# Two graph-attention layers on one core: one exponential per attention weight, two source tiles of ten as split one-pass products, and attention sums of `w2` moved one stage later

## The chip, the cores and the metric

The kernel runs on one core of a Trainium2 chip. The metric is the device time of one execution in microseconds (us), the median over several runs; lower is better. The engines are TensorE (PE, with its weight loads shown apart as PEld), VectorE (DVE), ScalarE (ACT), GpSimd (POOL) and SyncE (SP, here only a DMA queue).

## The reference, cut to what matters

A graph of 1250 nodes and 20000 edges plus a loop at each node passes two blocks, each followed by a layer normalization. The first block holds three attention convolutions of four heads with 192 features each:

```
h = (x1 @ W).reshape(N, H, C)                 # N=1250, H=4, C=192, three times
e = leaky_relu(as_n[src] + ad_n[dst], 0.2)    # as_n, ad_n: h times a_src, a_dst, summed
p = exp(e - segment_max(e, dst))
out = segment_sum(p / segment_sum(p, dst) * h[src], dst) + b
x = layernorm(x + relu(concat(relu(out)) @ W_out + b_out))
```

The second block is one such convolution of four heads with 512 features (weights `w1`), an ELU and one of a single head (weights `w2`).

## The kernel before

Nodes stand in `NT = 10` tiles of `T = 125`. The edge list has been turned into a dense matrix of counts `CT` (source by destination), so an aggregation over edges is a dense product: for each head and each source tile, a matrix `p` of 125 sources by 1250 destinations is built and multiplied with the 125 rows of `h`. The stages run one after another, each a block with a barrier behind it: counts and `x1`, `project` (h and the scores, and for each head the rows `u`, `v` per destination), `aggregate_layer0`, `project_out_layer0`, then the same for the second block.

**`aggregate_layer0` (L897).** 6 iterations of 2 heads, 20 steps each, 120 steps in all; a step is one source tile `s` of one head `hh`.
- ACT (L1048 to L1052) writes two exponentials per step, of `u` plus a source column and of `v` plus a scaled source column, 1250 wide, into a ring of 4. It may run 4 steps ahead of `p`.
- DVE (L1086 to L1094) takes the larger of the two (L1088), waits for itself, then takes min with 1 and multiplies by the counts into `p`, also a ring of 4 (L1093). Exponentials of two exponents, of which the larger is taken, are the leaky ReLU inside the exponential.
- PE (L1132 to L1143) multiplies: for each of 10 destination tiles a float32 product of 125x125 (stationary `p`) with 125x193 (193rd column of `h`: ones, which yields the sum of `p`). Such a product is recorded as two matmuls. The results of one head fill 5 PSUM banks, two destination tiles each. There is no second set of banks.
- So at each change of heads: DVE reads the sums and inverts them (`divisors`, L1071, called after step 1 of the next head, first for two banks and then for three), ACT scales the 10 results out of PSUM (`leave_head`, L1012, after the exponentials of step 3), and PE's first products of the next head wait for the bank. After two heads PE transposes the results in three chunks (`turn`, L1112, behind steps 1, 3 and 5 of the next iteration), ACT adds the bias (`keep`, L1025).
- In 16 of the first 110 steps, every seventh, DVE does two more reductions behind L1093: products of a chunk of `w2` (128 rows x 768) with the attention vectors of the last layer, summed (`ScoreWeights.reduce`, L634). POOL's queue loads these chunks.

**`project_out_layer0` (L1790).** 20 pieces (10 node tiles, two halves of the 18 chunks of 128), each 54 one-pass products of 384 columns with both operands split into a rounded part and a rest (float32r). Per piece ACT rounds and DVE forms the rest (`rest_of_f`, two buffers); per node tile DVE adds, normalizes (`leave`) and sums two or three chunks of `w1` with its attention vectors (`sums`, 24 chunks of 128x512 in a ring of 2, loaded by POOL's queue, the vectors once per 6 chunks).

Of the kernel before, what the change touches and what calls it, by code (L numbers as in the profile page):

```python
# [640 lines left out]
def project(nc, core, xT, w, wa, h_rows, score_rows, width, col_src, u_col, v_col):  # L641
# [12 lines left out]
    with ExitStack() as ctx:  # L654
# [111 lines left out]
        def _(dve):  # L766
# [5 lines left out]
            v.tensor_copy(col_src[0][:, 0:heads, :], score[:, 0])  # L772
# [124 lines left out]
def aggregate_layer0(nc, core, h_rows, col_src, bias, turned_rows, w2, a2, w_out):  # L897
# [9 lines left out]
    RING = 4  # L907
    with ExitStack() as ctx:
# [5 lines left out]
        e = sb("e", [T, RING, 2, N], F32)  # L914
        p = sb("p", [T, RING, N], F32)
        res = sb("res", [T, NT, PAIR], F32)
# [13 lines left out]
        more_ready = sem("more_ready")  # L930
        p_ready = sem("p_ready")
        p_used = sem("p_used")
        banks_done = sem("banks_done")
# [7 lines left out]
        weighed = ScoreWeights(nc, sb, sem, "wa2_by", 2, D // 2, 2, K1, K1, 1)  # L941
# [3 lines left out]
        def _(pool):  # L945
# [6 lines left out]
            by_half = w2.rearrange("(u g) (k p) c -> g k p u c", g=2, p=128)  # L952
            weighed.loads(pool, lambda n: by_half[n // (K1 // 2), n % (K1 // 2)],
                          lambda g: a2.rearrange("(u g) a c -> g u a c", g=2)[0:1].broadcast_to([128, 2, 2, D // 2]))
# [7 lines left out]
        def _(sp):  # L962
            sp.dma_start(b_col[:], bias).then_inc(bias_in, 16)

            def load(i):
                for s in range(2):
                    if (i, s) == (0, 0):
                        continue
                    wait_apart(sp, exp_ready, i * STEPS + (s + 1) * NT)
# [36 lines left out]
        def _(act):  # L1006
# [32 lines left out]
            def body(i, first):  # L1039
                for g in range(STEPS):  # L1040
                    hh, s = divmod(g, NT)
                    if s == 0:
                        if g == 0:
                            wait_apart(act, core.first_uv_in if first else uv_in[0], 64 if first else i * 64)
                        else:
                            wait_apart(act, uv_in[1], i * 64 + 64)
# [19 lines left out]
        def _(dve):  # L1066
            v = nc.vector
            v.sem_inc(p_ready, RING)
            v.sem_inc(exp_ready, 2 * NT)
# [12 lines left out]

            def body(i, first):
                for g in range(STEPS):
                    hh, s = divmod(g, NT)
                    dve.wait_ge(exp_ready, i * STEPS + (g + 1 + 2 * NT))  # L1086

                    v.tensor_tensor(e[:, g % RING, 0, :], e[:, g % RING, 0, :], e[:, g % RING, 1, :], ALU.max).then_inc(more_ready, 1)  # L1088
                    dve.wait_ge(more_ready, i * STEPS + (g + 1))

                    dve.wait_ge(p_used, i * STEPS + (g + 1 + 2 * NT - RING))

                    v.scalar_tensor_tensor(p[:, g % RING, :], e[:, g % RING, 0, :], 1.0, CT[:, s, :],  # L1093
                                           ALU.min, ALU.mult).then_inc(p_ready, 1)  # L1094
                    if (i * STEPS + g) % 7 == 4 and (i * STEPS + g) // 7 < K1:
                        k = (i * STEPS + g) // 7
                        weighed.reduce(dve, k, lambda kind, j: core.wa2[:, k, kind:kind + 1])
# [9 lines left out]
        def _(pe):  # L1107
# [16 lines left out]
            def body(i, first):  # L1124
                for g in range(STEPS):
# [6 lines left out]
                    pe.wait_ge(p_ready, i * STEPS + (g + 1 + RING))  # L1132
                    for d in range(NT):
                        b, n = divmod(d, 2)
                        if s == 0 and n == 0:

                            pe.wait_ge(bank_free, i * (2 * BANKS) + (BANKS * hh + b + 1))
                        last = nc.tensor.matmul(p_o[:, b, n * 256:n * 256 + C0 + 1], p[:, g % RING, d * T:(d + 1) * T],  # L1138
                                                h_in[hh][:, s, 0:C0 + 1], start=(s == 0 and n == 0), stop=(s == NT - 1),
# [650 lines left out]
def project_out_layer0(nc, core, turned_rows, w, x, bias, x2_rows, w1, a1):  # L1790
# [9 lines left out]
    with ExitStack() as ctx:  # L1800
# [129 lines left out]
        def _(dve):  # L1930
# [750 lines left out]
```

## Time and profile before

| | us |
|---|---|
| median of 3 runs | 1923.69 (1923.25 to 1928.69) |
| profiled execution, its own time | 1930.16 |
| its span | 1928.4 |
| PE busy | 1839.7 (95%) |
| DVE busy | 1443.6 (75%) |
| ACT busy | 1030.9 (53%) |
| POOL busy | 142.1 (7%) |

The span counts from the first to the last instruction that was recorded; the time holds some microseconds around it. Matmuls overlap, so that their duration says less than the distance from the start of one to the start of the next. "Idle before" an engine's instruction comes with the instruction that released it.

### The profile page before, as it was taken

The numbers are of one execution on the slowest core, as the hardware profiler recorded it, in microseconds if no ns is written. First come the engines' busy times: TensorE is split into PE (matmuls) and PEld (weight loads), VectorE is DVE, ScalarE is ACT, GpSimd is POOL, SyncE is SP. The second block draws the span as 40 slices with busy tenths as digits, with TensorE's granted clock in tenths as the row PEclk, the third lists the DMA queues.
The fourth block names the chain that finished last, engine by engine and source line by source line (L and its number), as shares of the span: only waits on it lengthen the run. The fifth ranks groups of instructions, "written<-read, shape, count | busy, mean of one in ns | idle before, by whom it ended". The sixth has DMA issues, their size and how long they took to land. (4 is left out here: it accounts for less than half of the span.)

```text
span 1928.4 us, 30682 instructions
## 1 busy us (share of the span) xinstructions
PE 1839.7 (95%) x11399; PEld 1776.6 (92%) x11399; DVE 1443.6 (75%) x2468; ACT 1030.9 (53%) x1634; POOL 142.1 (7%) x139
## 2 busy tenths in 40 slices
PE   7999999998999999998999999989999998999998
PEld 5877699998999999988999999989999998999997
DVE  8888599998888988965465549457888886346766
ACT  4676412218898889864211322257778875232632
POOL 5100211201000000000111011100000000000000
PEclk9999999999999999999999999989999999999989
DMA  4221335355455436619644466462342406544302
GB/s 126 67 64 54 99 103 149 101 133 142 134 111 131 108 77 149 145 16 248 185 141 143 135 208 188 141 193 79 108 143 66 138 28 204 156 129 126 99 9 80
DMA packets 179273, 234.12 MB, mean 121 GB/s; under 512 B 75943, under 2 KB 151655, under 8 KB 178889
## 3 DMA queue, kind: packets, MB, share of 16 engines
q1 hardware_dynamic: 170407, 202.98, 38.5%
q0 software_dynamic: 7984, 27.24, 4.9%
q10 hardware_dynamic: 748, 2.10, 0.4%
q8 instruction: 86, 1.41, 0.3%
q14 instruction: 48, 0.39, 0.1%
HBM read 167.27 MB, written 65.00 MB: 120 GB/s over the span
## 5 line engine op out<-in xcount | busy, mean ns | idle before, releaser
L1755 PE MATMUL p_o<-p_hi,h_parts 125*128 125x416 f32 (+1 forms) x960 | 283.0, 356 | 7.4 <-DVE z L1676 6.1
L1138 PE MATMUL p_o<-first_room,p 125*125 125x193 f32 x1200 | 202.2, 329 | 6.2 <-ACT res L1020 2.9
L1138 PEld LDWEIGHTS p_o<-first_room,p 125*125 125x125 f32 x1200 | 197.1, 189 | 8.0 <-issue 6.7
L1138 PE MATMUL p_o<-h_in,p 125*125 125x193 f32 x1200 | 200.9, 330 | 3.6 <-ACT res L1020 3.6
L1138 PEld LDWEIGHTS p_o<-h_in,p 125*125 125x125 f32 x1200 | 198.7, 190 | 5.0 <-issue 3.8
L1755 PEld LDWEIGHTS p_o<-p_hi,h_parts 125*128 125x128 f32 x960 | 182.0, 190 | 13.7 <-DVE z L1676 10.1
L781 DVE CUSTOM_DVE_ANT_0 max_junk<-src_row,G 125x1250 bf16<-125x1250 f32 x120 | 184.8, 1612 | 3.6 <-ACT src_row L819 1.5
L885 PE MATMUL p_h<-pw_hi,x1T 128*125 128x384 f32 x720 | 187.3, 341 | 0.0
L1088 DVE TENSOR_TENSOR e<-e 125x1250 f32<-125x1250 f32 x120 | 174.3, 1453 | 17.2 <-ACT e L1050 17.1
L1474 PE MATMUL p_h<-pw_hi,x2T 128*125 128x256 f32 (+1 forms) x960 | 177.8, 287 | 3.9 <-DVE h_out L1430 3.9
L1093 DVE SCALAR_TENSOR_TENSOR p<-e,CT 125x1250 f32<-125x1250 f32 x120 | 175.3, 1461 | 5.7 <-PE p_o L1138 1.7
L1755 PE MATMUL p_o<-p_lo,h_parts 125*128 125x416 f32 (+1 forms) x480 | 169.9, 354 | 0.0
L1050 ACT ACTIVATE e<-first_room,col 125x1250 f32<-125x1250 f32 x120 | 151.1, 1344 | 6.9 <-DVE p L1093 5.5
L1474 PEld LDWEIGHTS p_h<-pw_hi,x2T 128*125 128x125 f32 x960 | 150.4, 190 | 4.2 <-DVE h_out L1430 4.1
L1050 ACT ACTIVATE e<-uv,col 125x1250 f32<-125x1250 f32 x120 | 149.0, 1349 | 1.2 <-DVE p L1093 1.2
L1474 PE MATMUL p_h<-pw_lo,x2T 128*125 128x256 f32 (+1 forms) x480 | 136.9, 285 | 0.0
L885 PEld LDWEIGHTS p_h<-pw_hi,x1T 128*125 128x125 f32 x720 | 131.7, 188 | 1.2 <-issue 1.2
L2012 PE MATMUL p_y<-fw_hi,f_hi 128*125 128x384 f32 x360 | 121.9, 339 | 4.2 <-DVE fw_lo L1935 4.1
L885 PE MATMUL p_h<-pw_lo,x1T 128*125 128x384 f32 x360 | 122.5, 340 | 0.0
L2012 PE MATMUL p_y<-fw_lo,f_hi 128*125 128x384 f32 x360 | 121.6, 338 | 0.0
L2012 PE MATMUL p_y<-fw_hi,f_lo 128*125 128x384 f32 x360 | 121.5, 337 | 0.0
L481 PE MATMUL p_count<-src_hot,dst_hot 125*125 125x416 bf16 (+1 forms) x588 | 112.7, 350 | 6.3 <-DVE dst_hot L286 6.3
(285 smaller groups left out, 3839.3 us busy)
## 6 DMA issues: line engine op xcount, KB each, us to landing
f_raw<-turned SPq DMA_DIRECT2D x40, 500.0 KB, 8.8
h_parts<-h_rows SPq DMA_DIRECT2D x40, 448.0 KB
turned<-tail_room SPq DMA_DIRECT2D x18, 625.0 KB, 6.9
G<-turned SPq DMA_DIRECT2D x20, 562.5 KB
h_rows<-tail_room SPq DMA_DIRECT2D x22, 424.4 KB
h_rows<-h_out SPq DMA_DIRECT2D x16, 560.0 KB
h_rows<-tail_room SPq DMA_DIRECT2D x14, 560.0 KB
first_room<-in_w_gat POOLq DMA_DIRECT2D x36, 192.0 KB, 2.7
```

The source lines that it names most:

```text
L481: last = nc.tensor.matmul(p_count[:, i, 0:w], dst_hot[:, h, :], src_hot[:, h, a:a + w], start=False, stop=False, skip_group_check=True)
L781: v.tensor_tensor_reduce(out=junk[:, t % 2, :], in0=src_row[:, h % 2, :], in1=G[:, t, :], scale=1.0, scalar=NO_EDGE, op0=ALU.subtract, op1 ...
L885: last = nc.tensor.matmul(p_h[:, (u * NT + t) % 4, 0:width], xp[:, k, at], wp[:, u, k, :], start=(k == 0 and n == 0), stop=(k == KD - 1 an ...
L1050: last = a.activation(e[:, g % RING, kind, :], uv[hh][:, kind, :], ACT.Exp, bias=col_src[kind][:, bass.ds(i * 2 + hh, 1), s])
L1088: v.tensor_tensor(e[:, g % RING, 0, :], e[:, g % RING, 0, :], e[:, g % RING, 1, :], ALU.max).then_inc(more_ready, 1)
L1093: v.scalar_tensor_tensor(p[:, g % RING, :], e[:, g % RING, 0, :], 1.0, CT[:, s, :], ALU.min, ALU.mult).then_inc(p_ready, 1)
L1138: last = nc.tensor.matmul(p_o[:, b, n * 256:n * 256 + C0 + 1], p[:, g % RING, d * T:(d + 1) * T], h_in[hh][:, s, 0:C0 + 1], start=(s == 0 ...
L1474: last = nc.tensor.matmul(p_h[:, n % 4, 0:width], xp[:, k, at], wp[:, q % 2, k, 0:width], start=(k == 0 and j == 0), stop=(k == KD - 1 and ...
L1755: last = nc.tensor.matmul(p_o[:, bank(n, c), 0:w], h[:, s, kind, cols].bitcast(F32R), pp[:, g % RING, 0:w], start=(s == 0 and j == 0), sto ...
L2012: last = nc.tensor.matmul(p_y[:, t % 2, half, 0:CW], fp[:, n % 2, kk, :], wp[:, k, cols], start=(k == 0 and j == 0), stop=(k == KO - 1 and ...
```

## The change

- In `aggregate_layer0` DVE takes the larger exponent before the exponential: `larger_exponent(n)` adds the source column to `u` and takes the larger of that and `v` in one instruction, two steps ahead of `p` (`AHEAD = 2`). ACT then does one exponential per step, in place. The column of `u` is scaled by 1 - SLOPE in `project`, and the exponential's bias is the column times SLOPE.
- For source tiles 4 and 8 of each head the product is made of float32r parts: ACT rounds `p` and these two tiles of `h`, DVE subtracts, and PE does three products of 194 columns in the place of one float32 product.
- The sums over `w2` leave this stage. They are done in `project_out_layer0`: 32 chunks of 128x384 in two halves, in a ring of 2, four chunks per node tile from tile 1 to 8, with one instruction at the end that adds the halves. POOL's queue loads them in turn with those of `w1`.

```diff
-            v.tensor_copy(col_src[0][:, 0:heads, :], score[:, 0])
+            v.tensor_scalar(col_src[0][:, 0:heads, :], score[:, 0], 1 - SLOPE, None, ALU.mult)
...
@@ aggregate_layer0, scalar
-                    wait_apart(act, p_ready, i * STEPS + (g + 1))
-                    for kind in range(2):
-                        last = a.activation(e[:, g % RING, kind, :], uv[hh][:, kind, :], ACT.Exp,
-                                            bias=col_src[kind][:, bass.ds(i * 2 + hh, 1), s])
-                    last.then_inc(exp_ready, 1)
+                    wait_apart(act, larger, i * STEPS + (g + 1 + 2 * NT))
+                    a.activation(e[:, g % RING, :], e[:, g % RING, :], ACT.Exp,
+                                 bias=col_src[1][:, bass.ds(i * 2 + hh, 1), s]).then_inc(exp_ready, 1)
+                    n = i * STEPS + g
+                    if in_parts(n - 1) is not None:
+                        m = in_parts(n - 1)
+                        if m >= 2:
+                            act.wait_ge(p_used, step_in_parts(m - 2) + 1 + 2 * NT)
+                        act.wait_ge(p_ready, n + RING)
+                        a.activation(p_hi[:, m % 2, :], p[:, (n - 1) % RING, :], ACT.Copy).then_inc(p_hi_ready, 1)
+                    if s == 1:
...
+                        a.activation(h_hi[:, hh], h_in_parts(hh), ACT.Copy).then_inc(h_hi_ready, 1)
@@ aggregate_layer0, vector
+            def larger_exponent(n):
...
+                dve.wait_ge(p_ready, n + 1)
+                v.scalar_tensor_tensor(e[:, n % RING, :], uv[hh][:, 0, :], col_src[0][:, i * 2 + hh, s:s + 1], uv[hh][:, 1, :],
+                                       ALU.add, ALU.max).then_inc(larger, 1)
...
-                    dve.wait_ge(exp_ready, i * STEPS + (g + 1 + 2 * NT))
-                    v.tensor_tensor(e[:, g % RING, 0, :], e[:, g % RING, 0, :], e[:, g % RING, 1, :], ALU.max).then_inc(more_ready, 1)
-                    dve.wait_ge(more_ready, i * STEPS + (g + 1))
+                    dve.wait_ge(exp_ready, i * STEPS + (g + 1))
                     dve.wait_ge(p_used, i * STEPS + (g + 1 + 2 * NT - RING))
-                    v.scalar_tensor_tensor(p[:, g % RING, :], e[:, g % RING, 0, :], 1.0, CT[:, s, :],
+                    v.scalar_tensor_tensor(p[:, g % RING, :], e[:, g % RING, :], 1.0, CT[:, s, :],
                                            ALU.min, ALU.mult).then_inc(p_ready, 1)
-                    if (i * STEPS + g) % 7 == 4 and (i * STEPS + g) // 7 < K1:
-                        k = (i * STEPS + g) // 7
-                        weighed.reduce(dve, k, lambda kind, j: core.wa2[:, k, kind:kind + 1])
+                    if i * STEPS + g + AHEAD < ITERS * STEPS:
+                        larger_exponent(i * STEPS + g + AHEAD)
+                    n = i * STEPS + g
+                    if in_parts(n - 1) is not None:
+                        m = in_parts(n - 1)
+                        dve.wait_ge(p_hi_ready, m + 1)
+                        v.tensor_tensor(p_lo[:, m % 2, :], p[:, (n - 1) % RING, :], p_hi[:, m % 2, :].bitcast(F32),
+                                        ALU.subtract).then_inc(p_split, 1)
+                    if s == 2:
+                        dve.wait_ge(h_hi_ready, i * 2 + hh + 1)
+                        v.tensor_tensor(h_lo[:, hh], h_in_parts(hh), h_hi[:, hh].bitcast(F32), ALU.subtract).then_inc(h_split, 1)
@@ aggregate_layer0, tensor
+                        if m is None:
...
+                        else:
+                            for pp, hp in ((p_hi, h_hi), (p_hi, h_lo), (p_lo, h_hi)):
+                                last = nc.tensor.matmul(p_o[:, b, n * 256:n * 256 + HC0], pp[:, m % 2, nodes], hp[:, hh, m % EACH, :],
+                                                        start=False, stop=False, skip_group_check=True)
@@ project_out_layer0, gpsimd
+            pool.wait_ge(w_split, KO)
+            for t in range(1, NT):
+                for n in w1_chunks(t):
...
+                for m in w2_chunks(t, 0, 4):
...
+                    if m >= 2:
+                        pool.wait_ge(w2_summed, 2 * (m - 1))
+                    pool.dma_start(w2_ring[:, m % 2], w2[2 * half + k // (K1 // 2), k % (K1 // 2) * 128:(k % (K1 // 2) + 1) * 128, :]
+                                   ).then_inc(w2_in[m % 2], 16)
@@ project_out_layer0, vector
             for t in range(2, NT):
                 rest_of_f(2 * t)
                 sums(t - 1)
+                sums_of_w2(t - 1, 0, 2)
                 rest_of_f(2 * t + 1)
                 leave(t - 1)
+                sums_of_w2(t - 1, 2, 4)
             sums(NT - 1)
             leave(NT - 1)
+            dve.wait_ge(w2_summed, 4 * K1)
+            v.tensor_tensor(core.wa2[:], core.wa2[:], wa2_half[:], ALU.add)
```

## Rows read from the trace of the kernel before

**Rows 1.** The page, part 1: busy us, share of the span, instructions.
```profile
PE 1839.7 (95%) x11399; PEld 1776.6 (92%) x11399; DVE 1443.6 (75%) x2468; ACT 1030.9 (53%) x1634; POOL 142.1 (7%) x139
```

**Rows 2.** Stretches: first aggregation, a stretch inside it, output projection.
```profile
core 0: us, PE busy (x) PEld busy (x) DVE busy (x) ACT busy (x) POOL busy (x), PEclk, DMA share, GB/s
...
479.00:484.00 5.00, 5.00 (x17) 5.00 (x16) 4.93 (x5) 5.00 (x9) 0.00 (x0) 0.50 1.04 253
...
881.00:1078.00 197.00, 192.20 (x1096) 191.09 (x1097) 109.58 (x237) 46.43 (x55) 19.49 (x28) 1.00 0.56 169
438.00:862.00 424.00, 415.45 (x2550) 411.79 (x2550) 375.07 (x350) 353.56 (x396) 12.12 (x17) 0.99 0.47 113
```

**Rows 3.** Costliest groups of the first aggregation: count, busy us, mean ns, idle before.
```profile
L1138 PE MATMUL p_o<-first_room,p 125*125 125x193 f32 x1200 | 202.2, 329 | 6.2 <-ACT res L1020 2.9 <-issue 2.9 <-DVE p L1093 0.5
...
L1093 DVE SCALAR_TENSOR_TENSOR p<-e,CT 125x1250 f32<-125x1250 f32 x120 | 175.3, 1461 | 5.7 <-PE p_o L1138 1.7
...
L634 DVE CUSTOM_DVE_ANT_1 wa_by_junk<-wa_by_w,wa_by_a 128x768 bf16<-128x768 f32 x32 | 29.3, 952 | 2.6 <-DMA wa_by_w<-in_w 2.6
```

**Rows 4.** Timeline of engines: start us, us, instructions merged; transposes, and float32 products undisturbed.
```profile
520.71 1.23 PE L1120 MATMUL p_t<-ident,res 125*128 125x125 f32 x10
...
639.82 10.46 PE L1138 MATMUL p_o<-h_in,p 125*125 125x193 f32 x63
```

**Rows 5.** Timeline of the last stage: 256 columns, then weight loads of 2-column products.
```profile
1851.79 0.51 PE L2532 MATMUL p_ol<-h_lo_l,p_hi_l 125*125 125x256 f32 x3
1852.14 0.51 PE L2532 MATMUL p_ol<-h_hi_l,p_lo_l 125*125 125x256 f32 x3
...
1855.58 1.18 PEld L2540 LDWEIGHTS p_ol<-ones_l,G 125*125 125x125 f32 x10
```

**Rows 6.** Instructions of L2540: duration ns, min/median/max.
```profile
L2540 PEld LDWEIGHTS p_ol<-ones_l,G x20: 185/189/190, 1855.6 to 1897.2; 125*125 125x125 f32 x20
```

**Rows 7.** DVE's timeline in an undisturbed stretch of the first aggregation.
```profile
482.02 1.46 DVE L1093 SCALAR_TENSOR_TENSOR p<-e,CT 125x1250 f32<-125x1250 f32 x1
483.40 1.45 DVE L1088 TENSOR_TENSOR e<-e 125x1250 f32<-125x1250 f32 x1
484.89 1.46 DVE L1093 SCALAR_TENSOR_TENSOR p<-e,CT 125x1250 f32<-125x1250 f32 x1
```

**Rows 8.** DVE groups by form, whole span: scalar from a constant, from a column.
```profile
L1698 DVE SCALAR_TENSOR_TENSOR e<-e,CT 125x416 f32<-125x416 f32 x80 | 47.4, 593 | 2.8
...
L1683 DVE SCALAR_TENSOR_TENSOR tail_room<-z,b_col,tail_room 128x416 f32<-128x416 f32 x28 | 18.1, 646 | 0.0
```

**Rows 9.** Timeline of the first aggregation's start.
```profile
433.93 12.39 ACT L1050 ACTIVATE e<-first_room,col 125x1250 f32<-125x1250 f32 x10 [1.25 <-DVEq L1068]
...
438.03 1.46 DVE L1093 SCALAR_TENSOR_TENSOR p<-e,CT 125x1250 f32<-125x1250 f32 x1
...
439.59 6.65 PE L1138 MATMUL p_o<-first_room,p 125*125 125x193 f32 x29 [2.85 <-issue]
```

**Rows 10.** Timeline of the first change of heads, with `w2` sums in DVE's queue.
```profile
475.38 0.95 DVE L634 CUSTOM_DVE_ANT_1 wa_by_junk<-wa_by_w,wa_by_a 128x768 bf16<-128x768 f32 x1
...
477.13 0.16 DVE L1077 TENSOR_SCALAR sums<-p_o 125x4 f32<-125x4 f32 x1
...
478.48 7.71 PE L1138 MATMUL p_o<-h_in,p 125*125 125x193 f32 x29 [3.56 <-ACT res L1020]
```

**Rows 11.** Timeline of PE: a wait inside a head, and a later change of heads.
```profile
458.31 1.90 PE L1138 MATMUL p_o<-first_room,p 125*125 125x193 f32 x10 [0.47 <-DVE p L1093]
...
584.06 4.16 PE L1138 MATMUL p_o<-first_room,p 125*125 125x193 f32 x24 [0.96 <-ACT res L1020]
```

**Rows 12.** DVE's timeline in the output projection, three of its waits and the reductions.
```profile
990.28 1.33 DVE L1939 TENSOR_TENSOR f_lo<-G,f_hi 128x1125 fp32r<-128x1125 f32 x1 [3.58 <-ACT f_hi L1904]
...
1000.88 0.69 DVE L634 CUSTOM_DVE_ANT_1 tail_room<-tail_room 128x512 bf16<-128x512 f32 x1 [6.83 <-DMA tail_room<-in_a]
...
1003.36 0.96 DVE L1950 TENSOR_TENSOR p_y<-p_y,tail_room 125x768 f32<-125x768 f32 x1
...
1007.85 0.16 DVE L1973 SCALAR_TENSOR_TENSOR ln_shift<-ln_moments,ln_better 125x1 f32<-125x1 f32 x1
...
1019.30 0.69 DVE L634 CUSTOM_DVE_ANT_1 tail_room<-tail_room 128x512 bf16<-128x512 f32 x1 [5.39 <-DMA tail_room<-in_w]
```

More of the change, by code:

```diff
@@ L907, in aggregate_layer0 @@
     RING = 4
+    AHEAD = 2
+    IN_PARTS = (4, 8)
+    EACH = len(IN_PARTS)
     with ExitStack() as ctx:
@@ L913, in aggregate_layer0 @@
         uv, h_in = (uv_first, uv_other[:]), (h_first, h_other[:])
-        e = sb("e", [T, RING, 2, N], F32)
+        e = sb("e", [T, RING, N], F32)
         p = sb("p", [T, RING, N], F32)
+        p_hi = sb("p_hi", [T, 2, N], F32R)
+        p_lo = sb("p_lo", [T, 2, N], F32R)
+        h_hi = sb("h_hi", [T, 2, EACH, HC0], F32R)
+        h_lo = sb("h_lo", [T, 2, EACH, HC0], F32R)
         res = sb("res", [T, NT, PAIR], F32)
@@ L929, in aggregate_layer0 @@
         exp_ready = sem("exp_ready")
-        more_ready = sem("more_ready")
+        larger = sem("larger")
         p_ready = sem("p_ready")
         p_used = sem("p_used")
+        p_hi_ready = sem("p_hi_ready")
+        p_split = sem("p_split")
+        h_hi_ready = sem("h_hi_ready")
+        h_split = sem("h_split")
         banks_done = sem("banks_done")
@@ L951, in _, with in_parts, step_in_parts, h_in_parts @@
                            core.h0_late)
-            by_half = w2.rearrange("(u g) (k p) c -> g k p u c", g=2, p=128)
-            weighed.loads(pool, lambda n: by_half[n // (K1 // 2), n % (K1 // 2)],
-                          lambda g: a2.rearrange("(u g) a c -> g u a c", g=2)[0:1].broadcast_to([128, 2, 2, D // 2]))
+        def in_parts(n):
+            return n // NT * EACH + IN_PARTS.index(n % NT) if n % NT in IN_PARTS else None
+        def step_in_parts(m):
+            return m // EACH * NT + IN_PARTS[m % EACH]
+        def h_in_parts(hh):
+            return h_in[hh][:, IN_PARTS[0]:IN_PARTS[-1] + 1:IN_PARTS[1] - IN_PARTS[0], :]
         def every_iteration(eng, body):
@@ L968, in load @@
                         continue
-                    wait_apart(sp, exp_ready, i * STEPS + (s + 1) * NT)
+                    wait_apart(sp, larger, i * STEPS + (s + 1) * NT)
                     wait_apart(sp, p_used, i * STEPS + (s + 1) * NT)
@@ L1068, in _ @@
             v.sem_inc(p_ready, RING)
-            v.sem_inc(exp_ready, 2 * NT)
+            v.sem_inc(larger, 2 * NT)
             def divisors(i, hh):
@@ L1081, in divisors @@
                     v.reciprocal(sums[:, 1, 2 * b0:2 * b1], sums[:, 0, 2 * b0:2 * b1]).then_inc(sum_steps, 1)
+            def larger_exponent(n):
+                i, g = divmod(n, STEPS)
+                hh, s = divmod(g, NT)
+                if s == 0:
+                    if n == 0:
+                        dve.wait_ge(core.first_uv_in, 64)
+                    else:
+                        dve.wait_ge(uv_in[hh], i * 64 + 64 * hh)
+                dve.wait_ge(p_ready, n + 1)
+                v.scalar_tensor_tensor(e[:, n % RING, :], uv[hh][:, 0, :], col_src[0][:, i * 2 + hh, s:s + 1], uv[hh][:, 1, :],
+                                       ALU.add, ALU.max).then_inc(larger, 1)
+            for n in range(AHEAD):
+                larger_exponent(n)
             def body(i, first):
@@ L1832, in project_out_layer0 @@
         w1_in = sem("w1_in")
+        w2_in = [sem(f"w2_in{r}") for r in range(2)]
+        a2_in = sem("a2_in")
+        w2_summed = sem("w2_summed")
+        w1_chunks = lambda t: range(weighed.chunks * (t - 1) // (NT - 1), weighed.chunks * t // (NT - 1))
+        w2_chunks = lambda t, a, b: range(4 * (t - 1) + a, 4 * (t - 1) + b) if t < NT - 1 else ()
         block = ctx.enter_context(nc.Block())
@@ L1975, in sums, with sums_of_w2 @@
             def sums(t):
-                for n in range(weighed.chunks * (t - 1) // (NT - 1), weighed.chunks * t // (NT - 1)):
+                for n in w1_chunks(t):
                     weighed.reduce(dve, n, lambda kind, j: core.wa1[:, n % KD, kind, n // KD:n // KD + 1])
+            def sums_of_w2(t, a, b):
+                for m in w2_chunks(t, a, b):
+                    half, k = divmod(m, K1)
+                    if k == 0:
+                        dve.wait_ge(a2_in, 16 * (half + 1))
+                    dve.wait_ge(w2_in[m % 2], 16 * (m // 2 + 1))
+                    for kind in range(2):
+                        if 2 * m + kind:
+                            dve.wait_ge(w2_summed, 2 * m + kind)
+                        to = (core.wa2 if half else wa2_half)[:, k, kind:kind + 1]
+                        v.tensor_tensor_reduce(out=w2_junk[:], in0=w2_ring[:, m % 2], in1=a2_now[:, kind], scale=1.0, scalar=0.0,
+                                               op0=ALU.mult, op1=ALU.add, accum_out=to).then_inc(w2_summed, 1)
             rest_of_f(0)
```

58 lines of the change are left out of this document (42 added, 16 removed).

## The prediction

> **What bounds the kernel now.** I read the page first: PE is busy for 95% of the span, DVE for 75% [rows 1]. Then the stretches. The first aggregation (438 to 862 us) is PE's: 2550 matmul records fill 415 of 424 us, while DVE is busy for 375 us, 88% of it [rows 2]. DVE is second by so little that what it does late shows up in PE. Where it does, I took from the idle time before L1138 and from the timeline around each place:
> - a product step (one source tile) is 20 records. 63 records last 10.46 us, less the last one's 0.33 this is 10.13/62 = 0.1634 us per record, 3.27 us per step [rows 4]. 120 steps are 392 us, and 15 groups of transposes of (1.23 - 0.27) x 10/9 = 1.07 us are 16 us more [rows 4].
> - DVE's step is 1.38 us from L1093 to L1088 and 1.49 from L1088 to L1093, since the second waits for the first, 2.87 in all [rows 7]; per head 28.7, with two divisors of 0.35 each 29.4, and the `w2` sums, 16 x 1.8 us over 12 heads, another 2.4: 31.8 against PE's 32.7 in a head without transposes.
> - the `w2` sums fall where they hurt. At 475.38 two of them stand ahead of the divisors; ACT can't empty a bank, and PE idles 3.56 us [rows 10]. The clock falls behind it: from 479 to 484 us it is granted at 0.50, 1.2 GHz, and 17 records stand where 31 would [rows 2], 14 x 0.1634 = 2.3 us in that stretch, about 2.8 with its edges. At 458.31 PE waits 0.47 for `p`, and at three changes of heads (584.06 is one) 0.96 [rows 11].
>
> **The products in parts.** Removed in 24 steps: 20 records, 3.27 us. Added: 30 products of 194 columns, each with its own weight load of 125 columns. The trace has no such product. From above: 256 columns, also one pass, start 0.35/3 = 0.118 us apart [rows 5]. From below by the columns: the same scaled by 194/256 is 0.089. But weight loads have a pace of their own: ahead of products with only 2 columns, ten loads take 1.18 us, less one duration of 0.19 this is 0.99/9 = 0.110 us each [rows 5, 6]. Two columns can't hold anything up, so this is the load. I take 0.109: 30 x 0.109 = 3.27 us, and 24 steps give 0. Ends: 0.118 gives +0.27 x 24 = +6.5, 0.089 gives -0.60 x 24 = -14.4, of which DVE lets through what follows below.
>
> The Trainium skill has a rule for either side ("TensorE: Matmul & The Clock Gate"). Its section on the back-to-back issue gap puts a warm product at N/2.4 + 2.5 ns, for 194 columns 83 ns; that would be 2.50 us per step and -18 us. Its section on LDWEIGHTS puts a load at P/1.2, 104 ns for 125 columns. The 0.110 of the row speaks for the second as the floor here.
>
> **The larger exponent.** Removed: L1088, 120 x 1.45 us, and the wait behind it. Added: a two-operand instruction of the same 1250 elements with its scalar from a column. With a column L1683 takes 646 ns where L1698 with a constant takes 593, both 416 elements [rows 8]: +0.05. So 1.38 + 0.05 = 1.43 per step, and `p` 1.38: 2.81 where it was 2.87. The bounds are 1.38 and 1.49 for either instruction. ACT drops from two exponentials of 1.24 us (12.39 for 10) [rows 9] to one, 150 us less, beside its work for the parts (24 x 1.3 for `p`, 12 x 0.5); ACT bounds nothing, so this is worth 0.
>
> **DVE's head after.** 10 x 1.38 + 10 x 1.43 + two rests of `p` of 1.38 + the rest of `h` (388 elements, by the 416 of [rows 8] 0.5) + divisors 0.7 = 32.1 us, against PE's 32.7 plainly and 35.9 with transposes. DVE and PE are all but equal in seven heads. Two chains decide:
> - At the change of heads the last divisors end 0.55 us after PE's last product. From there DVE has until PE's step 4 (13.1 us later) to do p2, l4, rest of h, p3, l5, p4, l6, p5, l7 and the rest of p4: 4 x 1.38 + 4 x 1.43 + 0.5 + 1.38 = 13.1, so it is late by 0.55 and some 0.1 of semaphore: 0.65, in five heads (heads with transposes have 2.1 us more; the seventh, in the first iteration, 0.15).
> - It reaches the next divisors after 10 p, 10 l, 2 rests of p, 1 of h: 31.4 us, at 31.95, plus 0.1; PE has done the first four products of step 9 at 32.7 - 6 x 0.327 + 0.65 (the wait above) = 31.4. Late by 0.5 in six or seven heads.
> Together 3.3 + 0.15 + 3.3 = about 7 us of new waits, between 0 (if the column costs nothing and waits overlap) and 13 + 7 (if `p` keeps the 1.49 of today: 10 x 0.11 = 1.1 per head more).
>
> **The first head.** Before: exponentials from 433.93, first `p` complete at 439.49, PE's first step at 439.59 [rows 9], a cold one (0.50 clock, about 1.75 us lost), so step 4 starts at 439.6 + 13.1 + 1.75 = 454.4. After: two larger exponents and `p`, 4.25 us: PE starts at 438.2. But the rest of p4 stands behind 8 l, 6 p and a rest of h: 11.5 + 8.3 + 0.5 + 1.4 = 21.7, at 455.6. Loss 1.2, less the 0.5 of [rows 11] and its neighbour: +0.6. PE idles there for 4.3 us less the cold 1.75; the clock may fall as it did behind the 3.56 of [rows 10]. Between 0 and 2.8, I take 1.4.
>
> **The `w2` sums leave.** Returned: 3.56 + 2.8 + 3 x 0.96, and smaller pieces beside them (0.2 each at four places, 0.5 to 0.7 at 458): 10.5 us in all, counted against the plain change of heads.
>
> **They arrive in the projection.** There 54 products take 192.2/1096 = 0.175 us each, 9.5 per piece, 19 per node tile [rows 2]. DVE has 110 us of work in 197. Per node tile: 2 x 1.25 (rest of f), 2.7 chunks x 1.23 (`w1`), 4.7 for `leave` (1003.36 to 1008.01), and new 8 sums of 384 elements; 512 take 0.69 and 768 0.95, so at most 0.55 each and 0.48 when they follow one another, 3.8 us [rows 3, 12]: 14.3. On top come waits for DMAs, 6.83 where the vectors are loaded, 5.39 where a third chunk is [rows 12]. In the worst tile 21 against 19, but `rest_of_f` has a buffer in hand, DVE stands 3.58 us idle ahead of it in other tiles [rows 12], and the next tile makes good. POOL's queue is in order: a chunk of `w2` waits behind one of `w1`, but two of each four are issued while DVE does `leave`. PE is not reached: 0, up to 5 if each landing is 2 us later. The 6.3 MB more in 197 us are 32 GB/s beside 169. At the stage's end one addition of 32 elements, 0.2, stands behind the last `leave`. The scaled column in `project` is as small as the copy: 0.
>
> **Sum.** 0 - 10.5 + 7 + 0.6 + 1.4 + 0.2 = -1.3 us. Against the profiled execution (1930.16, span 1928.4) this is 1928.9; the median of the runs shown stands 6.5 lower, so 1922.4, say 1922.5. A measurement of this kernel tells 0.3%, 5.8 us, from no change.
>
> **Rivals.**
> - *The loads are no floor* and 194 columns go at 0.089 to 0.091. PE's parts step is 0.55 to 0.6 shorter. Heads with transposes (5) give all, 5.5; the others are DVE's already and give 0.2 each: -6.5, 1916. For it: float32r loads were not seen alone. Against: 0.110 in [rows 5, 6]. By the Trainium skill's issue gap (same page as above, 83 ns) heads with transposes would give 7.7, 1914, by the same cap of DVE. Chance of this group 0.17.
> - *Column scalars cost nothing*: DVE's head is 31.5, the two waits shrink to 0.4 and 0.15: -3.5 more, 1919. Chance 0.10.
> - *DVE becomes the bound (slower)*: `p` keeps 1.49, or ACT's exponential, now only two steps ahead and behind a rounding of `p`, `leave_head` (3.2 us) or `keep`, comes late. It decides from 0.6 us more per head; at 1.1 us per head +13, 1936. Against: `p` no longer reads what DVE has just written. Chance 0.12.
> - *Columns and loads add up*, 0.118: +6.5, of which DVE's waits give back 2.5: 1926.5. Chance 0.08.
> - *The projection's DVE is late*: landings of 6 us and more, +5, 1927.5. Chance 0.06.
> - My forecast as worked out: 0.47, own range 1919 to 1927.
> The range of 1915 to 1932 leaves out the far end of the slower case and a corner of the first. Faster by over 0.3% is most of the first rival and part of the second: 0.23. Slower: the third and the edges of the next two, 0.17. Same 0.60.
>
> **What will show it.** Product starts in steps 4 and 8: 0.109 apart, or 0.09. No half-clock stretch at 477 to 484 and no reductions in the aggregation; PE waits at step 4 of heads without transposes, released by the rest of `p` (DVE), near 0.65; at their ends 0.5 for ACT's `res`. DVE busy above 90% of the stage, PE's stage as long as before within 4 us. The projection from 881 us on as long as before, DVE at some 140 of 197. The forecast is wrong if either the spacing is below 0.1 or DVE's step is above 2.87.

## The result and the profile after

The changed kernel takes 1935.01 us (median of 6 runs, 1933.55 to 1938.98), the one before 1925.36 beside it (6 runs, 1923.25 to 1928.69): ratio 1.005, 95% interval 1.0036 to 1.0064. It is slower, and 3 us above the top of my range. The profiled executions stand 8.9 us apart by their spans, 1937.3 against 1928.4.

The page of the changed kernel, span and part 1 (columns as in [rows 1]):

```profile
span 1937.3 us, 31268 instructions
...
PE 1843.8 (95%) x11639; PEld 1778.4 (92%) x11639; DVE 1487.5 (77%) x2569; ACT 927.0 (48%) x1550; POOL 147.2 (8%) x156
```

Its stretches, as in [rows 2]: the aggregation, the projection, and two short ones with the clock down.

```profile
438.00:862.00 424.00, 415.80 (x2790) 410.46 (x2790) 380.44 (x320) 251.32 (x314) 0.00 (x0) 0.99 0.41 97
882.00:1083.00 201.00, 193.98 (x1082) 192.02 (x1082) 141.47 (x360) 45.51 (x54) 37.71 (x62) 0.98 0.66 201
...
974.00:981.00 7.00, 5.93 (x19) 5.93 (x20) 6.28 (x17) 1.59 (x3) 1.95 (x3) 0.52 0.66 213
455.00:462.00 7.00, 6.30 (x30) 6.30 (x31) 6.25 (x5) 2.70 (x3) 0.00 (x0) 0.53 0.01 2
```

The aggregation's end did not move: its first product starts at 438.47 and its last at 861.84, where they stood at 439.59 and 861.63; my sum had it 1.5 us earlier. The projection did: its 1080 products start between 882.25 and 1082.82, 200.6 us, where they took 192.6 (881.33 to 1073.94). All later stages have the length they had. So of 8.9 us, 8.0 are the projection's; 0.2 are the aggregation's later end, and 0.7 lie between its last product and the projection's first.

Groups of the aggregation after, by form (columns as in [rows 3]):

```profile
L1132 DVE SCALAR_TENSOR_TENSOR p<-e,CT 125x1250 f32<-125x1250 f32 x120 | 174.3, 1453 | 7.1 <-PE p_o L1192 3.9 <-PE p_o L1197 2.6
...
L1120 DVE SCALAR_TENSOR_TENSOR e<-uv,col 125x1250 f32<-125x1250 f32 x60 | 90.8, 1514 | 0.0
...
L1197 PE MATMUL p_o<-h_hi,p_hi 125*125 125x194 f32 x240 | 69.0, 287 | 5.4 <-DVE p_lo L1140 5.4
```

The first head and its first step in parts (step 4), PE's timeline:

```profile
438.47 13.31 PE L1192 MATMUL p_o<-first_room,p 125*125 125x193 f32 x80 [1.63 <-issue]
455.70 0.53 PE L1197 MATMUL p_o<-h_hi,p_hi 125*125 125x194 f32 x1 [3.93 <-DVE p_lo L1140]
```

The place in the projection where most is lost: DVE's timeline (the rest of `f` at 935.62 with which the tile ahead begins, the two long waits behind it, the first sum of `w2`, the rest of `f` that comes late and the one that ends the tile), then PE's and POOL's.

```profile
935.62 1.33 DVE L2029 TENSOR_TENSOR f_lo<-G,f_hi 128x1125 fp32r<-128x1125 f32 x1
...
945.40 0.69 DVE L634 CUSTOM_DVE_ANT_1 tail_room<-tail_room 128x512 bf16<-128x512 f32 x1 [6.01 <-DMA tail_room<-in_w]
...
968.84 0.69 DVE L634 CUSTOM_DVE_ANT_1 tail_room<-tail_room 128x512 bf16<-128x512 f32 x1 [9.02 <-DMA tail_room<-in_a]
...
971.29 0.55 DVE L2080 CUSTOM_DVE_ANT_0 wa_junk<-tail_room,G 128x384 bf16<-128x384 f32 x1
...
973.68 1.33 DVE L2029 TENSOR_TENSOR f_lo<-G,f_hi 128x1125 fp32r<-128x1125 f32 x1
...
981.93 1.33 DVE L2029 TENSOR_TENSOR f_lo<-G,f_hi 128x1125 fp32r<-128x1125 f32 x1
```
```profile
975.07 0.68 PE L2120 MATMUL p_y<-fw_hi,f_hi 128*125 128x384 f32 x1 [3.82 <-DVE f_lo L2029]
```
```profile
960.12 0.56 POOL L1965 DMA_DIRECT2D tail_room<-in_a  x1 [9.46 <-DVE wa L634]
```

How to read it: POOL may ask for the next vectors only when DVE has done the last chunk of the old ones, at 960. They land 9 us later, DVE stands still, then does two chunks of `w1`, four of `w2`'s reductions (971.29 to 973.7) and only then the rest of `f` (973.68), for which PE has waited since 971. The vectors' wait itself is not new: in the kernel before the same sum waits 9.12 us and PE never notices,

```profile
964.33 0.69 DVE L634 CUSTOM_DVE_ANT_1 tail_room<-tail_room 128x512 bf16<-128x512 f32 x1 [9.12 <-issue]
```

which the view puts down to "issue", that is, to nothing that it could name. What is new is how DVE stands to PE. Before, the rest of `f` behind this wait was done at 968.1, 1.8 us ahead of PE's tenth piece (969.9). In the changed kernel the reductions have used up what DVE was ahead, and it is done at 975.0, after PE has stood for 3.8 us. From 935.62 to 981.93 it goes through two node tiles with three chunks of `w1` each: 46.3 us, 31.3 of work and 15.0 of waits (6.01 and 9.02), where PE takes 38.0 for two tiles. The wait for the tenth piece and the clock behind it lengthen two pieces, 9.5 us otherwise, to 13.5 and 12.3: 6.8 of the 8.0 us. The next such pair (998.31 to 1042.35, 44.0 us) costs PE a wait of 0.7.

From 974 to 981 the clock is granted at 0.52, 1.2 GHz for nearly all of it: 19 records, with 1.1 us of the wait among them, where 40 go at 2.4 GHz. By the granted clock it stays down for 6.8 us.

What the prediction should have been built on is one view, DVE's groups in a stretch of the projection, 920 to 1070 us. First the kernel before:

```profile
L634 DVE CUSTOM_DVE_ANT_1 tail_room<-tail_room 128x512 bf16<-128x512 f32 x48 | 30.5, 688 | 32.1 <-DMA tail_room<-in_w 16.1 <-issue 9.1 <-DMA tail_room<-in_a 6.8
L1939 DVE TENSOR_TENSOR f_lo<-G,f_hi 128x1125 fp32r<-128x1125 f32 x16 | 21.3, 1331 | 31.7 <-ACT f_hi L1904 31.6
```

and the changed one:

```profile
L2080 DVE CUSTOM_DVE_ANT_0 wa_junk<-tail_room,G 128x384 bf16<-128x384 f32 x60 | 33.5, 558 | 3.4 <-issue 0.2
L634 DVE CUSTOM_DVE_ANT_1 tail_room<-tail_room 128x512 bf16<-128x512 f32 x42 | 26.7, 687 | 29.7 <-DMA tail_room<-in_w 13.3 <-DMA tail_room<-in_a 9.0 <-issue 7.4
L2029 DVE TENSOR_TENSOR f_lo<-G,f_hi 128x1125 fp32r<-128x1125 f32 x16 | 21.2, 1327 | 4.0 <-ACT f_hi L1994 4.0
```

DVE's idle time before had two kinds. 31.6 us in 8 tiles is waiting for ACT's rounding, which follows PE: that is slack, time that DVE could work without holding anything up, 3.95 us a tile. The other 32 us is waiting for `w1`'s transfers (the 9.1 put down to "issue" is the wait shown above, 9.02 in the changed kernel) with the rest of `f` queued behind: no slack, though DVE is idle. The change spent the slack (4.0 left) and kept the waits (29.7).

### The profile page after: what moved, and what is told of

Its sections match the earlier page's. It is cut to its first block and busy times, and to the rows that moved or that the text cites. A ratio compares the mean times of both kernels' runs of the same rounds, so it can differ in the third digit from the quotient of the medians.

```text
span 1937.3 us, 31268 instructions
## 1 busy us (share of the span) xinstructions
PE 1843.8 (95%) x11639; PEld 1778.4 (92%) x11639; DVE 1487.5 (77%) x2569; ACT 927.0 (48%) x1550; POOL 147.2 (8%) x156
## 5 line engine op out<-in xcount | busy, mean ns | idle before, releaser
L1063 ACT ACTIVATE e<-e,col 125x1250 f32<-125x1250 f32 x120 | 160.2, 1340 | 135.3 <-DVE e L1120 135.2
L1132 DVE SCALAR_TENSOR_TENSOR p<-e,CT 125x1250 f32<-125x1250 f32 x120 | 174.3, 1453 | 7.1 <-PE p_o L1192 3.9
L1192 PE MATMUL p_o<-first_room,p 125*125 125x193 f32 x960 | 162.2, 328 | 4.0 <-ACT res L1040 2.3
L1192 PE MATMUL p_o<-h_in,p 125*125 125x193 f32 x960 | 161.2, 328 | 0.0
L1192 PEld LDWEIGHTS p_o<-first_room,p 125*125 125x125 f32 x960 | 156.2, 188 | 5.5 <-issue 5.5
L1192 PEld LDWEIGHTS p_o<-h_in,p 125*125 125x125 f32 x960 | 156.4, 188 | 1.5 <-ACT res L1040 1.4
L2404 PE MATMUL p_y<-fw_hi,f_hi 128*125 128x386 f32 x320 | 109.2, 341 | 7.5 <-DVE f_lo L2298 6.8
L284 DVE TENSOR_SCALAR src_hot<-node_no,edge_col 125x1250 bf16<-125x1250 int16 x196 | 103.8, 560 | 15.7 <-PE p_count L481 13.2
```

Of the source, the lines that this page charges most:

```text
L284: hot = v.tensor_scalar(src_hot[:, h, :], node_no[:], edge_col[:, 0, h, at], None, ALU.is_equal)
L1063: a.activation(e[:, g % RING, :], e[:, g % RING, :], ACT.Exp, bias=col_src[1][:, bass.ds(i * 2 + hh, 1), s]).then_inc(exp_ready, 1)
L1132: v.scalar_tensor_tensor(p[:, g % RING, :], e[:, g % RING, :], 1.0, CT[:, s, :], ALU.min, ALU.mult).then_inc(p_ready, 1)
L2404: last = nc.tensor.matmul(p_y[:, t % 2, 0:CW + 2], fp[:, m % 2, kk, :], wp[:, k, :], start=(k == 0 and j == 0), stop=(k == K1 - 1 and j == 2))
```

## The experiments

"PE's pace" below is the time from the first product of the sixth piece to that of the twentieth in the projection: 132.7 us before, and the same in every kernel whose PE never waits there; 140.3 in the changed kernel. The changed kernel's projection, unaltered, gave 137.6, 138.3 and 137.1 in e2, e7 and e9 (202.1, 199.8 and 197.6 us for the whole stage): 137 to 140 is one and the same result. In all four it is the tenth piece that comes late; PE idles 2.5 to 3.8 us before it, and the clock stays down for 3.4 us behind it, 6.8 in the changed kernel's own trace. The first five pieces, ahead of this stretch, differ too: 50.9 to 55.2 us in these four. A stage is given from its first to its last product. Ratios are to the kernel before on the same chip.

**Which stage lost the time** (e1, e2). e1: the changed aggregation, the projection of before, `w2`'s sums left out altogether.

> The changed aggregation as it is; the output projection is that of the kernel before; the sums over w2 are left out altogether (zeros in their place), with their loads. Theory A (the loss is in the projection: DVE comes late with the rest of f, PE waits about 4 us once and the clock falls to half behind it; the aggregation alone is about even): the projection is back at 192.6 us from its first to its last product (before 192.6, changed 200.6), and the whole at 1925 to 1928, 0 to +2 us against the kernel before. Rival B (the aggregation costs the time, in the runs that are not profiled): still +7 or more, 1933.

1928.07 us, ratio 1.0009 (0.9996 to 1.0022); aggregation 425.0, projection 192.8, pace 132.7. e2: the other half, the aggregation of before without the sums, the changed projection with them.

> The aggregation of the kernel before without the sums over w2 and their loads, and the changed projection, which does them. Theory A: the aggregation returns its stalls at the first change of heads (3.7 us and the half clock behind it, 2.8), at three others (1.1 each) and 0.7 inside a head, 10 us in all; the projection pays 8: about -2 us against the kernel before, 1923. Rival B: the projection's loss depends on where the aggregation ends and does not show here: -8 or more.

1924.49 us, 0.9997 (0.9984 to 1.0009); aggregation 410.3, projection 202.1. The move alone gives 11.7 us in the one stage and loses 9.5 in the other. The loss is the sums' in the projection, whatever the aggregation is.

**DVE's work or POOL's transfers** (e3, e4). e3: `w2_ring[:, m % 2]` and `a2_now[:, kind]` cut to 2 of their 384 columns in the reduction, all loads kept.

> The changed kernel with all loads of w2 and its vectors, but each of the 64 reductions over 2 of 384 columns (the rest of the sum is left out): DVE's work for them falls from 3.8 us per node tile to about 1. Theory A1 (DVE's own work, 2.4 us between two rests of f, is what makes the rest late): the 4.2 us wait shrinks to under 2, the clock stays up, -5 to -7 us against the changed kernel. Theory A2 (the loads: the vectors of w1 land 9.0 us after DVE needs them, where it was 6.8): the wait stays above 3 us and the time within 2 us of the changed kernel.

1927.5 us, 1.0004 (0.9991 to 1.0017); projection 192.3, pace 132.7, with DVE's waits for `w1` as long as ever (920 to 1070 us):

```profile
L634 DVE CUSTOM_DVE_ANT_1 tail_room<-tail_room 128x512 bf16<-128x512 f32 x48 | 30.5, 687 | 29.3 <-DMA tail_room<-in_a 15.4 <-DMA tail_room<-in_w 13.8
```

e4: the reductions at full size, the loads only for `m < 2` and only the first of the two pairs of vectors; the sums are made of these again and again.

> The changed kernel with all 64 reductions of full length, but only the first two chunks of w2 and one pair of its vectors are loaded and used again and again (30 loads of chunks and one of vectors are left out). Theory A1 (DVE's work): the wait at the fifth node tile stays at 2 us or more, the time within 3 us of the changed kernel. Theory A2 (the loads and their order in POOL's queue): the vectors of w1 land as before (6.8 us wait), the rest of f is in time or under 2 us late, -5 to -8 us against the changed kernel.

1934.24 us, 1.0044 (1.003 to 1.0059); projection 199.4, pace 137.6. So DVE's reductions of `w2` are needed for the loss, and the 6.3 MB that they read are not; whether the reductions alone are enough is e13's question.

**Sums at chosen steps of the aggregation** (e5, e6). In both:

```
-   if (i * STEPS + g) % 7 == 4 and (i * STEPS + g) // 7 < K1:
+   if i * STEPS + g in W2_AT:   # h * NT + 4 for h in 1..11, h * NT + 7 for h in 2, 4, .. 10
```

e5 also has the larger exponent with one exponential, and no parts.

> The changed kernel's aggregation with one exponential for each weight, but without any parts (every product is of float32), and w2's attention sums back in the aggregation, at sixteen chosen steps (step 4 of heads 1 to 11, step 7 of heads 2, 4, 6, 8, 10) where PE has work in hand; the projection is the one of the kernel before. Theory A (the change lost its gain by putting the sums on VectorE inside the projection, and by the waits that the parts bring into the aggregation): VectorE's work in a head is 10 steps x (1.432 + 1.378) = 28.1 us and one or two reductions of some 1.75 us, below PE's 32.7 us for the 20 x 10 products of float32, so the first product to the last takes about 410 us (422.0 before, 423.4 changed), the projection 192.6 us, the whole 10 to 12 us less than before, about 1914 to 1916 us. Rival B (the sums cost 10 us wherever they stand, because the engine that they hold up is late whatever the step): aggregation 420 us or more, the whole within 3 us of before.

1918.16 us, 0.9964 (0.9948 to 0.998); aggregation 411.8, projection 192.3.

> The kernel before, in which only the steps change at which VectorE does w2's sixteen reductions in the aggregation: step 4 of heads 1 to 11 and step 7 of heads 2, 4, 6, 8, 10 in place of every seventh step. Nothing else is changed: both exponentials, the maximum and the product stay as they are. Theory A (what the sums cost in the kernel before is their place: one that falls at the end or beginning of a head, where VectorE also takes the head's end, holds PE up): first product to last in 411 to 413 us in place of 422.0, the whole 9 to 11 us less than before. Rival B (VectorE's step of about 2.9 us leaves too little beside PE's 3.27 us for any reduction): the aggregation takes 418 us or more and the whole changes by less than 4 us.

1915.36 us, 0.9946 (0.9928 to 0.9965), the fastest of all; aggregation 410.3, projection 192.5. PE's timeline where [rows 10] had a wait of 3.56 and a half clock, and the stretch:

```profile
472.50 13.76 PE L1139 MATMUL p_o<-h_in,p 125*125 125x193 f32 x82
```
```profile
439.00:851.00 412.00, 410.62 (x2550) 407.34 (x2550) 374.16 (x351) 352.92 (x397) 11.28 (x16) 1.00 0.47 116
```

DVE's step is still 2.87, ACT still does two exponentials, the clock is granted at 1.00 throughout. One condition is worth 11.7 us of this stage by the traces, as the sums' going altogether is in e2; 1.7 of it in both is not the sums' doing: in the kernel before's trace the stage begins with 3.4 us at a granted clock of 0.51, and in these two it doesn't. Some 10 us are the condition's, as the medians have it too (10.4); the single exponential adds nothing: e5's interval overlaps e6's, and its aggregation starts 1.3 us earlier (438.43 against 439.75) but ends where e6's does (850.25, 850.05), since PE waits 1.47 us for ACT's `res` at the first change of heads.

**What the parts cost** (e7, e9). e7: `in_parts` returns `None`, every product of float32.

> The changed kernel without the parts: every source tile's products are of float32, the copies, subtractions and three-pass products go; one exponential for each weight and the w2 sums in the projection stay. Theory A (the parts bring no shorter products and only waits): the aggregation from first product to last takes about 410 us in place of 423.4: 4 us of wait and 3 us of half clock in the first head go, and eleven waits of about 0.6 us. The projection keeps its 8 us of loss, 200 to 202 us, and the whole is 1921 to 1925 us. Rival B (the three one-pass products are shorter than the float32 one, and their going costs time): aggregation above 420 us and the whole at or above the changed kernel's time.

1921.42 us, 0.9972 (0.9954 to 0.999); aggregation 411.8, projection 199.8. Without the parts the stage is 11.6 us shorter. e9: parts from the second head on.

```
-   return n // NT * EACH + IN_PARTS.index(n % NT) if n % NT in IN_PARTS else None
+   return (n // NT - 1) * EACH + IN_PARTS.index(n % NT) if n >= NT and n % NT in IN_PARTS else None
```

> The changed kernel with the parts from the second head on only: the first head's ten source tiles are all of float32. Theory A (the parts cost by waits, and the first head's is the largest: PE waits 3.9 us at its step 4 and then has half the clock for 6.8 us): both go, the aggregation takes 416 to 418 us from first to last product in place of 423.4, with the 0.6 us waits of the later heads still there, and the whole is 5 to 8 us less than the changed kernel, 1927 to 1930 us. Rival (the first head's wait is only moved, and comes up at the first step in parts of the second head, with its clock): aggregation 421 us or more.

1927.6 us, 1.0017 (1.0002 to 1.0033); aggregation 416.5. The second head's step 4 comes without a wait:

```profile
471.36 13.31 PE L1189 MATMUL p_o<-h_in,p 125*125 125x193 f32 x80 [1.47 <-ACT res L1040]
484.37 0.39 PE L1194 MATMUL p_o<-h_hi,p_hi 125*125 125x194 f32 x1
```

So 6.9 of the 11.6 us go with the first head's parts, and 4.7 are left. The 6.9 are mainly the wait of 3.9 and the clock behind it, about 3. They are not exact: what is only one execution's clock counts in them. Behind the same wait of 3.93 us the clock stayed down for 6.8 us in the changed kernel, 3.4 in e10 and e12 and 10.2 in e1, and with it the same aggregation took 423.4, 421.9 and 425.0 us.

**Can order mend the projection** (e8, e10, e11, e12, e14). e8: `w1`'s chunks dealt 3, 3, 3, 3, 3, 3, 2, 2, 2, so that vectors are loaded at a tile's first chunk.

> The changed kernel with w1's chunks dealt to the projection's tiles so that the first chunk of each group of three, which needs the group's attention vectors loaded, is the first chunk of a tile (3, 3, 3, 3, 3, 3, 2, 2, 2 chunks) and not the second or third. The number of reductions is the same. Theory A1 (VectorE comes late to the rest of f at the ninth piece because its own work, one reduction of w2 for a tile more, and a wait of 9.0 us for vectors that were asked for too late, come together): with the vectors early, that wait of 9.0 us goes, PE's waits of 3.8 and 1.5 us with the half clock behind them shrink, projection 193 to 197 us in place of 200.6, the whole 4 to 8 us less than the changed kernel, 1927 to 1931 us. Rival A3 (VectorE's total work in a tile is too long by itself, wherever the vectors are): the projection stays at 199 to 202 us.

1942.88 us, 1.0091 (1.0059 to 1.0123), 8 us worse than the changed kernel, which neither theory had; projection 208.6, pace 146.0. No wait for vectors is left in the stretch, and waits for chunks took their place:

```profile
L634 DVE CUSTOM_DVE_ANT_1 tail_room<-tail_room 128x512 bf16<-128x512 f32 x44 | 28.0, 687 | 34.4 <-DMA tail_room<-in_w 34.4
```

e10: the rest of `f`'s second piece ahead of the tile's first two chunks of `w2`.

> The changed kernel in which VectorE, in each tile of the projection, makes the rest of f's second piece before the tile's first two w2 reductions and not behind them; the number of reductions is the same. Theory A (what costs 8 us is that two reductions of w2 stand ahead of a piece that PE comes to, in tiles where a third chunk of w1 is already waited for): the rest of f comes 2.4 us earlier at pieces 9, 13 and 15, PE's wait of 3.8 us shrinks to about 1.4 and the shorter ones go, projection 193 to 197 us in place of 200.6, the whole 4 to 8 us less than the changed kernel. Rival A3 (the sum of VectorE's work and its waits for transfers in a tile is too long, so the lateness goes to the first piece of the next tile): projection 199 us or more.

1931.44 us, 1.0036 (1.0022 to 1.005); projection 198.7, pace 137.5: near the rival's 199, and within what the unaltered projection gives. e11: the same order without parts.

> Both mendings in one: no parts (float32 products throughout, one exponential for each weight) and the rest of f's second piece ahead of the tile's first two w2 reductions. If the two losses of the changed kernel are separate and both mended, the aggregation takes 411.8 us and the projection 193 to 197, the whole 1914 to 1919 us, as the kernel of before with its sums at chosen steps (1915.4). If the projection's lateness is not mended by the order, it stays at 1921 us.

1922.15 us, 0.9984 (0.9969 to 0.9998), projection 199.5: no better than e7. e12: third chunk and all of `w2` behind the tile's end.

```
-   sums(t - 1); sums_of_w2(t - 1, 0, 2); rest_of_f(2 * t + 1); leave(t - 1); sums_of_w2(t - 1, 2, 4)
+   sums(t - 1, 0, 2); rest_of_f(2 * t + 1); leave(t - 1); sums(t - 1, 2, 3); sums_of_w2(t - 1, 0, 4)
```

> The changed kernel in which VectorE takes, in each tile of the projection, the third chunk of w1 (where there is one) and all four w2 reductions behind the tile's end, and not ahead of the rest of f's second piece. The same instructions, in another order: the 5 to 9 us waits for that third chunk's transfer then fall into a stretch in which VectorE has the tile's end to do. Theory W (what makes f late are the waits for w1's third chunk and for its vectors, in a queue of instructions that is otherwise about full: 3 chunks x 2.45 + 4 w2 reductions x 1.2 + the tile's end 4.6 + two rests of f x 1.24 = 19.2 us against PE's 19.1 for a tile): the waits shrink below 3 us each, projection 193 to 196 us in place of 200.6, the whole 5 to 8 us below the changed kernel, 1927 to 1930. Rival S (the work alone fills VectorE, waits or not): projection 198 us or more.

1936.19 us, 1.007 (1.0048 to 1.0093); projection 199.6, pace 139.3; and with no parts besides (e14)

> e12's order in the projection, and no parts in the aggregation (float32 products, one exponential for each weight). By theory W and what the kernel without parts gave: aggregation 411.8 us, projection 193 to 196 us, the whole 1914 to 1917 us. By rival S 1919 to 1922, as without the new order.

1924.41 us, 0.9989 (0.9976 to 1.0003); projection 202.9, pace 141.4: no gain either, and slower than both theories had it. One figure in e12's and e13's expectations is wrong: a chunk of `w1` is two reductions, 1.23 us and not 2.45, so a three-chunk tile is 3.7 + 4.8 + 4.6 + 2.5 = 15.6 us of work, not 19.2. So both results lie on rival S's side: this order did not mend the pace. But it did not remove the waits either: they shrank by less than 5 us (29.7 to 25.2) and else only moved, since a load's request is itself released by a sum in the same queue. So e12 can't tell W from S. e12's groups, 920 to 1070 us:

```profile
L2080 DVE CUSTOM_DVE_ANT_0 wa_junk<-tail_room,G 128x384 bf16<-128x384 f32 x56 | 31.3, 558 | 19.1 <-DMA tail_room<-in_w 16.8
L634 DVE CUSTOM_DVE_ANT_1 tail_room<-tail_room 128x512 bf16<-128x512 f32 x42 | 26.8, 687 | 9.5 <-DMA tail_room<-in_a 9.0 <-issue 0.5
```

**The waits taken away** (e13): `w1`'s loads only for `n < weighed.ring`, the first vectors alone, all reductions at full size on what lies there.

> The changed kernel without the loads of w1 chunks and vectors for its attention sums in the projection but the first two chunks and the first vectors; all 48 reductions of w1 run at full size on what lies there. Theory W (the waits make f late): without them VectorE's 19.2 us in a three-chunk tile and 16.8 in a two-chunk tile stay under PE's 19.1 on average, no rest of f is late by more than some tenths, projection 192.5 to 194.5 us, the whole 6 to 8 us below the changed kernel. Rival S (the work alone): 197 us or more.

1928.5 us, 1.0014 (1.0002 to 1.0026), 6.5 below the changed kernel; projection 195.3, pace 132.7. The whole stage is above W's 194.5 because of its start, where PE waits 2.6 us at 895.93 for `fw_lo` and the clock falls for 3.4 us; from the sixth piece on PE does not wait at all. DVE's groups in 920 to 1070 us:

```profile
L2081 DVE CUSTOM_DVE_ANT_0 wa_junk<-tail_room,G 128x384 bf16<-128x384 f32 x64 | 35.7, 558 | 3.4
L634 DVE CUSTOM_DVE_ANT_1 tail_room<-tail_room 128x512 bf16<-128x512 f32 x43 | 27.0, 685 | 0.0
L2030 DVE TENSOR_TENSOR f_lo<-G,f_hi 128x1125 fp32r<-128x1125 f32 x16 | 21.3, 1331 | 25.0 <-ACT f_hi L1995 25.0
```

The same work, more of it finished (64 against 60 reductions of `w2` in the stretch), and 25.0 us of slack. The work with the waits gone fits (e13), the waits with the work cut fit (e3, before), and the two together don't. That is the cause, shown from both sides. On average there is nothing to spare: about 15.2 us of work a tile and 4.0 of waits (29.7 over the 7.5 tiles that 150 us hold) against PE's 19.0. But the average doesn't make the loss. It falls where two tiles with three chunks and a long wait each stand one behind the other, 46.3 us against 38.0.

## Why the prediction was wrong

- **Products in parts: right.** L1197's starts are 0.109 us apart, thirty to a step as long as twenty of float32. The Trainium skill's rule for a weight load ("TensorE: Matmul & The Clock Gate", section "LDWEIGHTS (loading the stationary operand)"), 104 ns for 125 columns, is near this. The 83 ns that I took from the Trainium skill's section "Back-to-back issue gap" of the same page isn't seen. That section gives the formula for an isolated product and says that in a stream of weight loads and products both set the spacing; I had left this condition out.
- **Larger exponent: right.** 1.43 from L1120 to L1132 and 1.37 from there on, predicted 1.43 and 1.38; 1514 ns for one. ACT bounds nothing, as forecast: it stands for 132 us waiting for DVE's L1120.
- **New waits of the parts: right.** Six waits at step 4 cost 0.54 each above the plain spacing (0.65 predicted), five changes of heads 0.63 (0.5 predicted; its own terms, 31.95 + 0.1 - 31.4, make 0.65): 6.4 of "about 7". By e9 against e7 the later heads' come to 4.7.
- **First head: mechanism right, size off.** PE started at 438.47 (438.2) and reached step 4 at 455.70 (455.6), idle 3.93 (4.3). But the clock fell for 6.8 us, 30 records in 7 us where 64 go; I took 1.4 us between 0 and 2.8, it was about 3, and other executions of the same code lost half as much or half as much again. This is most of why the aggregation ended 0.2 us later and not 1.5 earlier.
- **`w2`'s sums leave: right.** 10.5 predicted; 11.7 in e2 and in e6, less the 1.7 of the clock at the stage's start, which my sum counted in the first head: 10.0.
- **They arrive in the projection, "PE is not reached: 0": the step that failed.** It was +8.0, beyond the "up to 5" I left open. Three of its readings were wrong.
  - The price. The eight reductions of a tile were priced at 0.48 each, 3.8 us; they start 0.60 apart (971.29 and its three successors to the rest of `f` in 2.4 us, the 0.08 of reading the sum behind each), so 4.8.
  - The slack. It was read from a busy share ("110 us of work in 197") and one idle row of 3.58 in tiles that had it. Grouped over 8 tiles it was 31.6 us, 3.95 per tile, against 8 x 4.8 = 38.4 needed: short by 6.8. That PE's pace lost 7.6 is near this in part by luck, since 2.8 of the 7.6 are the half clock behind the one long wait.
  - The overlap. I had written down waits for transfers [rows 12] and a worst tile of 21 us against 19, then let "the next tile makes good". But the longest wait, 9.12 us at 964.33, was not among my rows, so that the worst tile takes 24.7 us (957.27 to 981.93), and the tile ahead of it takes 21.7: what should make good was itself late.
- **The signs I had named** (spacing below 0.1, DVE's step above 2.87) both stayed away and the forecast was wrong all the same; only the projection's length, of the things listed under "What will show it", told of the loss.
- **The rival that came nearest** was "the projection's DVE is late", 0.06 by chance, with landings of 6 us and more as its condition and +5 as its price. Its place was right. As a condition, later landings were not needed: the longest waits are as long as before (9.02 and 6.01 against 9.12 and 5.66), and e4 without `w2`'s transfers loses as much. But waits of that length were half of the cause, as e13 shows, which loses nothing without them.

## What to carry to other kernels

Before work is moved onto an engine that is "55% busy", split its idle time by what ends it: waiting for the bounding engine is slack, waiting for a transfer with the bounding engine's input queued behind is not. Compare the slack with the whole pitch of what is added, accumulator reads too, and not on the mean alone: find the longest wait and the two worst periods in a row. An idle time put down to "issue" can be such a wait. And first try to move work within its stage: one condition on the steps gave 10 us (0.9946) where the whole change lost as much.

## What the runs showed of the chip

- One-pass products of 194 columns, each with its own weight load of 125 columns, start 0.109 us apart, as loads ahead of products of 2 columns do (0.110), so the load sets this pace; splitting a float32 product in three saved nothing: 30 x 0.109 = 20 x 0.163.
- PE waits of 3.8 and 3.9 us in the middle of a stage were followed by half clock (974, 455); waits of 0.5 to 1.5 us at changes of heads (e9's 1.47) were not. In between it varied: behind 2.52 us in e9 the clock fell, behind 2.96 us in e11 (963.77) it didn't.
- How long it stays down varies between executions too: behind the same wait of 3.93 us in the first head it was 3.4, 6.8 or 10.2 us (e10 and e12, the changed kernel, e1), and the stage took 421.9, 423.4 or 425.0. A difference of 3 us in one stage's trace is not yet a result.
- A ring of two chunks whose loads are released by the consumer's own sums held 25 to 34 us of waits in 150 in each order tried (32.1 before, 29.7 changed, 34.4 in e8, 28.6 - 3.4 = 25.2 in e12, where 3.4 is what the pairs of reductions have between them without any wait).
